# Down products of a shared network in 128-token tiles, residual rows by DMA, and another seam to the experts

## What is computed

```python
n = layernorm(h)                              # (6016, 256)
scores = softmax(n @ gate_w.T).T              # (16, 6016)
w, idx = top_k(scores, C)                     # C = 752 tokens for each of 16 experts
g, u = xg @ Wg.T, xg @ Wu.T                   # xg = n[idx], per expert, 1024 wide
eo = ((gelu(g) * u) @ Wd.T) * w
out = zeros.at[idx].add(eo)
shared = (gelu(n @ Sg.T) * (n @ Su.T)) @ Sd.T # 512 wide, for all tokens
h = h + out + shared
```

## Time and profile before

| | |
|---|---|
| runs | 1777.65, 1777.69, 1775.45 us; median 1777.65 |
| profiled execution | 1777.74 us, span 1775.9 us |
| TensorE busy | 1645.1 us, 93% of the span, mean granted clock 0.966 |
| VectorE, ScalarE, GpSimd busy | 1217.5, 936.1, 1009.8 us |
| chain that ended last | TensorE 77%, VectorE 5%, issue 5% |
| down products of the shared network (L1671) | 768 matmuls |
| small products of the one-hot stage (L1711) | 1024 |

### The profile page before, as it was taken

The page is one execution under the profiler, slowest core; times in us unless marked ns, Lnnn a source line. Parts: engine busy times, 40 slices in busy tenths (PEclk is TensorE's granted clock), DMA queues, the critical chain, the costliest instruction groups (busy, mean ns, idle before and its releaser), DMA issues.

```text
span 1775.9 us, 47092 instructions
## 1 busy us (share of the span) xinstructions
PE 1645.1 (93%) x15406; PEld 1232.7 (69%) x15406; DVE 1217.5 (69%) x3827; ACT 936.1 (53%) x2160; POOL 1009.8 (57%) x1069
## 2 busy tenths in 40 slices
PE   5883999999999997799997699999999999999997
PEld 5882666777777764577776377777777777777775
DVE  3884888999999997857796555555555555555541
ACT  3553767777777775542334544444444444444432
POOL 3772355566666655722242346667666666766665
PEclk9895999999999998999998699999999999999999
DMA  6541455666666663420010524344333334333322
GB/s 186 162 137 43 120 140 135 149 152 148 151 147 148 147 145 95 118 53 28 28 36 20 180 88 107 104 107 105 103 101 101 93 94 107 88 99 93 91 33 30
DMA packets 173652, 186.82 MB, mean 105 GB/s; under 512 B 119544, under 2 KB 146680, under 8 KB 167416
## 3 DMA queue, kind: packets, MB, share of 16 engines
q1 hardware_dynamic: 138488, 135.03, 27.0%
q0 software_dynamic: 35072, 50.62, 13.9%
HBM read 134.59 MB, written 50.44 MB: 104 GB/s over the span
## 4 chain that ended last, share of the span: by engine, by line
PE 77%; DVE 5%; issue 5%; SPq 4%; POOL 3%; ACT 2%; DMA 2%; DVEq 0%; POOLq 0%; ACTq 0%
PE psum L1798 28%; PE psum L1815 14%; PE psum L1651 6%; PE psum L1524 5%; PE psum L1671 4%; PE psum L1493 3%; PE psum L1535 3%; PE psum L1505 3%; SPq L484 3%; PE psum L1479 3%; PE psum L1557 2%; PE psum L1546 2%; POOL hidden L590 2%; POOL arena L595 1%; PE psum L1778 1%
## 5 line engine op out<-in xcount | busy, mean ns | idle before, releaser
L666 POOL TENSOR_TENSOR arena<-arena 128x376 f16<-128x376 f32 x320 | 315.1, 987 | 354.3 <-ACT arena L769 352.9
L1798 PE MATMUL psum<-arena,hidden 128*128 128x376 f16 x3072 | 493.8, 323 | 0.9 <-DVE arena L1400 0.9
L1798 PEld LDWEIGHTS psum<-arena,hidden 128*128 128x128 f16 x3072 | 301.2, 98 | 189.5 <-issue 2.3
L769 ACT ACTIVATE arena<-arena 128x376 f16<-128x376 f32 (+5 forms) x610 | 284.6, 474 | 63.2 <-DVE arena L1327 47.1
L993 ACT ACTIVATE arena<-psum 128x376 f32<-128x376 f32 x256 | 123.7, 483 | 342.9 <-PE psum L1798 342.9
L1149 DVE CUSTOM_DVE_ANT_0 arena<-psum,constants 128x188 f32<-128x188 f32 x768 | 237.6, 347 | 53.9 <-PE psum L1479 44.1
L1410 DVE SCALAR_TENSOR_TENSOR arena<-psum,arena 128x376 f32<-128x376 f32 x256 | 140.7, 550 | 181.6 <-ACT arena L993 180.1
L1815 PE MATMUL psum<-hidden,arena 128*128 128x256 f16 (+1 forms) x2304 | 256.6, 273 | 0.0
L769 ACT ACTIVATE arena<-psum 128x188 f32<-128x188 f32 (+7 forms) x457 | 176.1, 398 | 150.6 <-PE psum L1778 58.0
L1815 PEld LDWEIGHTS psum<-hidden,arena 128*128 128x128 f16 (+1 forms) x2304 | 230.3, 103 | 21.4
L818 ACT ACTIVATE arena<-psum 128x376 f32<-128x376 f32 x384 | 184.2, 481 | 81.5 <-PE psum L1493 80.6
(11 more groups left out here) (159 smaller groups left out, 2730.6 us busy)
## 6 DMA issues: line engine op xcount, KB each, us to landing
arena<-e_g SPq DMA_DIRECT2D x16, 1024.0 KB
arena<-e_u SPq DMA_DIRECT2D x16, 1024.0 KB, 5.0
arena<-e_d SPq DMA_DIRECT2D x16, 1024.0 KB
arena<-x_t SPq DMA_DIRECT2D x32, 376.0 KB, 3.4
weighed<-arena POOLq DMA_DIRECT2D x32, 376.0 KB, 3.8
arena<-q_halves SPq DMA_DIRECT2D x192, 47.0 KB, 3.2
arena<-k_halves SPq DMA_DIRECT2D x96, 94.0 KB, 2.3
arena<-q_halves SPq DMA_DIRECT2D x96, 94.0 KB, 2.2
```

The source lines that it names most:

```text
L666: nc.gpsimd.tensor_tensor(dst, f, hi, ALU.subtract).then_inc(ready, 1)
L769: return nc.scalar.activation(dst, src, ACT.Copy, scale=scale)
L1798: last = mm(bank[2 * (s % 2) + i][:, 0:CHUNK], w_, a, start=n == 0, stop=n == 5)
```

## The change

Down products of the shared network go by 47 tiles of 128 tokens. A tile may straddle two chunks, so the halves `SHH` and `SHL` become rings of 896 (7 x 128) tokens for each of the four hidden quarters, and an operation that crosses the ring's end is written as two. Tile j is made in the step that `down_step` gives: three of four steps have one, the first of a chunk has none. Each tile has a PSUM bank of its own in turn (4 or 5). As `H` holds tiles of 94 tokens, each tile's residual rows are copied by two or three DMAs into one of three buffers `RES` (`residual`), three tiles ahead; the addition waits for it (`res_in`), and each tile is stored by one DMA.

The score table is treated in `NJ` = 6 pieces of up to 128 columns instead of 8 of 94: one-hot operations are 128x192, six value copies a quarter, 192 small products a quarter. Of the last quarter VectorE makes two value scalings itself (`last_values`).

In the seam: at step 40 SP loads the first expert's gate weights and half of its up weights into the space of weights that are no longer needed, the other half at step 52. ScalarE converts them in steps 41 to 46, 55 and 59 (`high_first`), GpSimd makes the low halves in steps 53 to 60 (`low_first`). Quarter 0 is multiplied a step earlier, quarter 1 straight after the last step, ahead of the last three down tiles, quarters 2 and 3 behind them. VectorE turns quarters 0 and 1 into lists ahead of the last quarter's one-hots. The first expert's down weights are converted within its own steps, and the second half of the lists is made there too. The first gathered rows lie elsewhere in the arena and are turned in banks 4 and 5.

```diff
-NJ = CH // HT
+NJ = -(-CH // 128)
-QC = QE * 64
+QC = QE * 8 * NJ
+LOADS = 40
+ST = T // 128
+HRING = 7 * 128
+AHEAD = 3
+OUTS = 3
...
+        def down_step(j):
+            k = chunk_of(j)
+            return 4 * k + 5 + j - CHUNK * k // 128
...
+            def residual(j):
+                for tile, row, to, n in residual_parts(j):
+                    sp.dma_start(RES[j % AHEAD][to:to + n, :], H[row:row + n, tile, :]).then_inc(res_in[j % AHEAD], 16)
+            def tile_out(j):
+                sp.wait_ge(sh_added, j + 1)
+                sp.dma_start(out[128 * j:128 * j + 128, :], SOUT[j % OUTS]).then_inc(sh_out[j % OUTS], 16)
+                if j + AHEAD < ST:
+                    residual(j + AHEAD)
...
+                if s == LOADS:
+                    sp.wait_ge(y_added, B)
+                    sp.dma_start(W0[0], e_g[0, :, 0:1536]).then_inc(w_first_in, 16)
+                    sp.dma_start(W0[1][:, 0:512], e_g[0, :, 1536:2048]).then_inc(w_in[0], 16)
+                    sp.dma_start(W0[1][:, 512:1536], e_u[0, :, 0:1024]).then_inc(w_first_in, 16)
+                if s == HOT:
+                    sp.wait_ge(slots, 18)
+                    sp.dma_start(PSC, e_u[0, :, 1024:2048]).then_inc(w_in[1], 16)
...
+            def low_first(p):
+                i, h = divmod(p, 4)
+                pool.wait_ge(sh_added, -(-44 * HT // 128))
+                pool.wait_ge(wh_ready[i], 2 * h + 2)
+                c = slice(512 * p, 512 * p + 512)
+                nc.gpsimd.tensor_tensor(WEL[0][:, c], FIRST_ST[p], WEH[0][:, c], ALU.subtract).then_inc(wl_ready[i], 1)
...
+                if HOT + 1 <= s < HOT + 9:
+                    low_first(s - HOT - 1)
...
+            first_steps = [LOADS + 1 + p for p in range(6)] + [HOT + 3, HOT + 7]
+            def high_first(p):
...
+                copy(WEH[0][:, 512 * p:512 * p + 512], FIRST_ST[p], WSCALE).then_inc(wh_ready[i], 1)
+                copy(FIRST_ST[p], FIRST_ST[p], WSCALE).then_inc(wh_ready[i], 1)
...
+            def down_out(j):
+                dve.wait_ge(down_done, j + 1)
+                dve.wait_ge(res_in[j % AHEAD], residuals_in(j))
+                if j >= OUTS:
+                    dve.wait_ge(sh_out[j % OUTS], 16 * (j // OUTS))
+                nc.vector.scalar_tensor_tensor(SOUT[j % OUTS], bank[4 + j % 2][:, 0:D], 1.0 / (WSCALE * HSCALE), RES[j % AHEAD],
+                                               ALU.mult, ALU.add).then_inc(sh_added, 1)
...
+                for j in downs_at(s - 1):
+                    down_out(j)
...
-            down_out(KS - 2, 1)
-            for n in range(STEPS - HOT, STEPS - HOT + 2):
-                hot_part(n)
-            dve.wait_ge(hf_ready, STEPS)
             tokens_of_slots(0)
             list_half(0, (0,))
-            for n in range(STEPS - HOT + 2, 4 * E // QE):
+            for j in downs_at(STEPS - 1):
+                down_out(j)
+            for n in range(STEPS - HOT, 4 * E // QE):
                 hot_part(n)
-            down_out(KS - 1, 0)
-            down_out(KS - 1, 1)
+            last_values()
+            for j in range(ST - 3, ST):
+                down_out(j)
             list_half(0, (1, 2, 3))
...
+                    if first and s == 0:
+                        tokens_of_slots(1)
+                    if first and s in (1, 2):
+                        list_half(1, (2 * s - 2, 2 * s - 1))
+                    if first and 3 <= s < 7:
+                        low_expert(0, 2, s - 3, 0)
...
+            def down(j):
+                pe.wait_ge(hl_ready, 4 * chunk_of(j) + 4)
+                pe.wait_ge(lsub_done, min(j, 1) + 1)
+                if j >= 2:
+                    pe.wait_ge(sh_added, j - 1)
...
-                if s >= 5:
-                    down(s - 5)
+                for j in downs_at(s):
+                    down(j)
...
-                if s == HOT + 8:
+                if s == HOT + 7:
                     hot_quarter(0)
-            for n_ in range(STEPS - 5, STEPS):
-                down(n_)
-            for q in range(1, E // QE):
+            hot_quarter(1)
+            for j in range(ST):
+                if down_step(j) >= STEPS:
+                    down(j)
+            for q in range(2, E // QE):
                 hot_quarter(q)
...
-            pe.wait_ge(slots, 25)
+            pe.wait_ge(sh_added, ST)
             token_transposes(0, 0, range(4))
```

## The result

The changed kernel takes 1760.14 us (median of four, 1755.51 to 1760.71), the kernel before, run beside it on the same chip, 1776.78. The ratio is 0.9901 [0.9882, 0.9920]: 16.6 us faster, where 25.2 were forecast. The profiled span is 1758.9 us against 1775.9. The moment at which step 8 of the shared network starts differs between them by up to 3.6 us (754.4 to 758.0). Most of that arises in stages that the change doesn't touch (the network's first step starts between 705.5 and 710.5), so lengths of stages are compared and not moments.

What follows compares the result with a forecast made beforehand. TensorE was taken to bound the shared network's steps, VectorE chains next, then a 48.7 us seam. Gains 13.1 (loop) + 14.6 (seam) - 2.5 (first expert) = 25.2 us, from 1777.74 to 1752.5; 8-in-10 range 1743 to 1767.

Steps and rivals of the forecast that it cites:

- The seam: From the last step's end to the first expert's start: 34.1 us instead of 48.7, 14.6 gained, bounds 8.9 and 16.8.
- The search: Steps 15 to 44: eight down groups less, 10.5 us, of which 4.2 given back to VectorE's chain; 6.3 gained.
- the one-hot stage: Steps 52 to 63: 40.7 us instead of 42.8, about 1.0 lost per step to GpSimd collisions; 2.1 gained.
- The loop: The shared network's steps together: 13.1 us gained, bounds 5.3 and 20.9.
- (a): Rival in which VectorE loses nearly every collision with GpSimd: 1769.5 us; chance 0.14.
- Steps 5 to 14: Early shared network: three down groups less at 1.31 us each, all 3.9 us gained as VectorE has half its time free.
- The priced wait: In search steps without a down product, the small product waits 0.5 us for VectorE's chain; eight times, 4.2 given back.
- Steps 45 to 51: One down group less, 1.3 us, beside VectorE's long scans; 0.8 gained.
- The walk: Event-by-event timing of the seam from the last step's end: tile 44's addition at 16.3, transposes and tokens done at 34.1.
- The gather: GpSimd's gathers in the seam: rows there at 31.8, needed at 29.2, yet no cost taken; bound 2.6 us.
- rival (c): Additions wait for residual copies requested three tiles earlier, making the kernel slower: 1781.5 us; chance 0.05.
- The first expert: It takes over VectorE work (slot sums, listing, four weight conversions): 2.5 us lost, bounds 0 and 6.

Runs made afterwards that it cites:

- the repeat: The changed kernel run again unaltered, beside three edits of it on the same chip: 1759.99 us, 0.9910 of the kernel before.

## Why the prediction was right, and where not

The sign and the range held (1760.14 in 1743 to 1767); the gain was 16.6 us instead of 25.2. The seam's part came by the mechanisms that it named. The search's nearly vanished by one that it hadn't, and the one-hot stage's came out smaller. The loop gained 6.0 us, close to the lower bound of 5.3, and the time lies nearly midway between the forecast (1752.5) and the 1769.5 of (a), in which VectorE loses nearly every collision with GpSimd. That it still fell into the range is due to the range's width. Step by step, from the profiled executions:

- **Steps 5 to 14: 3.9 us.** Steps 8 to 15 gained 3.3, and the step ahead of them, from 2.38 us between two GELUs to 1.80, another 0.6: 3.9. A group of 128 tokens kept the 1.31 us of one of 94 (909.55 to 910.86). Right.
- **The search: 6.3 gained. The failed step.** Steps 15 to 45 gained 0.8. That in a step with a down product "the next small product is due 3.22 us after the last, and the chain hides" was wrong: the product itself waits, through the PSUM bank, for an addition behind that chain, and that wait comes in the step before the one I priced. The priced wait (0.5 in the step without a product) didn't occur at all, as the slack had been spent before. Of 1.31 us removed per four steps 0.31 was left, 7.5 x 0.31 = 2.3, less a single wait of 1.47 at 783.41 for the addition behind the first count (which waits for the score table in SP's queue): 0.8. (8 x 0.5 is 4.0 and not the 4.2 of the sum, which matters little.) When the addition was moved and the queue cleared, the priced wait appeared (0.27 and 0.34), the cycle was 12.74, and the stage gained 5.2 of the 6.3. My arithmetic was that of a kernel whose additions stand elsewhere. I had given "the output addition ahead of it" one clause, and had asked what the addition delays, never what waits for the addition.
- **Steps 45 to 51: 0.8.** 1.3 was seen. All of the group.
- **The one-hot stage: 2.1 gained.** From step 52 to the end of the loop (904.6 to 946.9) it took 42.3 us for 40.7 forecast and 42.8 before: 0.5 gained. In the repeat, at half the clock in step 59, it took 44.5. A term mis-sized: I gave each step about 1.0 us lost to GpSimd, for one or two neighbours; beside four in a row it was 3.3 (4.79 for 1.50) and 2.6 (4.58 for 1.97), and TensorE stood 3.29 behind it. Moving six of eight neighbours away gave 3.9 us in steps 52 to 59. The bounds (37.7 and 44.8) held for both. In the stretch of 4.79 the 3.3 were lost beside four neighbours of 4.0 together, so most of their length; at 911.65 GpSimd lost 1.4 instead (2.57 for 1.16).
- **The seam: 34.1 long.** 36.2 measured. The walk held part by part: last down product at +15.3 (16.3 in the walk) after 6.29 idle (some 7), its 2.65 us at half clock (2.6), 56 one-hots in 6.7 (6.9), transposes and tokens 4.95 (4.95). The 2.6 was my estimate, twice the 1.31 of a group, and no row of before shows a group of down products at a lower clock; in the changed kernel the group of 962.22 took those 2.65 us at a granted clock of 0.50. Mis-sized was the term for quarters 2 and 3, 13.3 instead of 10.2: I took 40 ns for the upper end of one quarter alone. With the loads held they take 11.0, so these make 2.3 us of it in this profile; the earlier gaps are the rest.
- **The gather.** The first took 6.85 us, until VectorE's one-hots and value scalings ended (961.7), where the next took 0.97, and the rows were still in time: no cost, as forecast.
- **The residuals, rival (c).** Right that they don't set the pace. Wrong that nothing waits for them: 1.36 us at 788.04 in the changed kernel, 5.38 once the cover was gone. "SP does nothing else in these 200 us than wait for additions" had overlooked its router block at step 12. The price was not the landing but the queue: 9.0 and 1.9 of waiting and 5.28 of issue. The copies also delay the score table's load; without them the search was 2.0 us shorter.
- **The first expert: 2.5 lost.** Its gate/up stage took 34.6 us (983.09 to 1017.68) for 33.0: 1.6 lost, with waits of 0.15, 0.53 and 0.85 for L1516 where the walk put them. Right in kind, 1.6 for 2.5.

Together 6.0 + 12.5 - 1.6 = 16.9 of the 17.0 by which the spans differ.

## What to carry to other kernels

When a product is removed from a pipeline, list for each step that gets shorter everything that its instructions wait for, PSUM banks in turn included, and look at where the release stands in the other engine's list: an addition written behind a long chain is as late as the chain. Two waits in a row hide each other. A run that removes one and gets slower doesn't refute it, so remove both, as 2.6 slower, 0.7 faster and 4.4 faster showed here. Work that is taken off a seam isn't free where it lands: GpSimd operations go where VectorE doesn't run one-hot operations in rows (3.9 us here), and big loads go where TensorE isn't issuing hundreds of tiny products (1.3 to 3.0 us here).

## What the runs showed of the hardware

- Twelve one-hots of 128x192 took 4.79 us instead of 1.50 while GpSimd ran four operations with no pause between; with gaps between them one of the two lost, VectorE 0.66 to 0.68 or GpSimd about 1.0.
- Runs of small products (24 columns) have gaps in issue. The one ahead of the last 114 ended 1.15 to 1.48 us after a 16 KB packet of the queue `q8 instruction` in nine kernels. It was 1.94 to 3.31 us in the six kernels that load 3 MB beside it in the changed kernel's order, 0.91 with these loads held back, and 1.72 and 1.44 in the kernels with the first weights in the seam and without the copies. The earlier gaps (0.47 to 1.19) didn't change with the loads held, and they were absent in those two. What makes them, the runs don't show.
- The same kernel had a granted clock of 0.83 in step 59 in one execution and 0.50 in another, and the step took 6.62 and 8.82 us.
- SP took 5.28 us to issue eight stores and 0.65 to 0.85 us for each residual copy (1.29 to 1.70 for two, 2.11 to 2.24 for three), so a queue of stores can be late by its issue alone.
